# An int8 stage between the quantising VectorE step and its bf16 result, in a macaron block of feed-forward, RWKV attention and feed-forward on eight cores

## The chip, the cores and the metric

The kernel runs on one Trainium2 chip, on 8 cores at once. Each core takes one batch element: 4096 tokens of 1024 channels. The metric is the device time of the slowest core in microseconds. Every time below is one of such runs, or is read from the trace of one profiled execution of the kernel before, on core 5, the slowest of it. A core has five engines that run side by side and wait for each other through semaphores: PE (TensorE, matmul), DVE (VectorE), ACT (ScalarE), POOL (GpSimd) and SP (SyncE, which only issues transfers here). "PEld" is PE's loading of weights.

## The reference, cut to what matters

```python
x = x + 0.5 * ffn(layernorm(x), w_gate, w_up, w_down)
x = x + attn(layernorm(x), w, u, mix_k, mix_v, mix_r, Wk, Wv, Wr, Wo)
x = x + 0.5 * ffn(layernorm(x), w_gate, w_up, w_down)      # same weights as the first

def _weight_quant(w):                  # one scale for the whole matrix, values -1, 0, 1
    scale = 1.0 / clip(mean(abs(w)), 1e-05)
    return clip(round(w * scale), -1.0, 1.0) / scale
def _act_quant(x):                     # one scale per token, values -127 to 127
    scale = 127.0 / clip(max(abs(x), axis=-1), 1e-05)
    return clip(round(x * scale), -128.0, 127.0) / scale
def _bitlinear(x, w):
    return einsum('bsi,oi->bso', _act_quant(x), _weight_quant(w))
def ffn(x, w_gate, w_up, w_down):      # 1024 -> 4096 -> 1024
    return _bitlinear(silu(_bitlinear(x, w_gate)) * _bitlinear(x, w_up), w_down)
```

The attention has four projections of 1024 x 1024, a shift by one token with three mixes, and a recurrence over the tokens (running maximum, numerator, denominator). The change doesn't touch it.

## The kernel before, in words

**Weight stage, once.** For each of the three feed-forward matrices (4 M elements) there are two passes in 4 blocks of 128 partitions x 8192 elements, with two buffers `wbat`. The first pass sums the absolute values (L238). The second pass loads the blocks again and quantises each in three DVE steps: scale and clip above (L272), clip below and add 12582912 (L276; at that size an fp32 number has no digits behind the point, so the addition rounds), subtract 12582912 and write bf16 into `bbat` (L282). ACT's queue stores `bbat` to scratch. SP loads block nb only when DVE is through with block nb-2 (`vdone`), since they share a buffer. After the four blocks the matrix is transposed by DMA from scratch to scratch.

**Main part, four times** (`q` = 0 to 3, 1024 tokens each, held in `xres`): `ffn(q)`, `attn(q)`, `ffn(q)`, with a barrier of all engines behind each. In `ffn` the 1024 tokens are two tiles (`tt`) of 512 tokens, each of them 4 groups (`sub`) of 128. The order is written out by hand:

```python
quant(0)
for t in range(NTT):
    gu(t)
    if t + 1 < NTT:
        quant(t + 1)
    rounds(t)
    down(t)
```

- `quant` does the layer norm (`ln_tile`: ACT squares at L326, the rest on DVE), the maximum per token (L398), the scaling (L418) and the rounding into bf16 `xqb3` (L420: add 12582912, subtract it). `xqb3` goes to scratch, and eight DMA transposes bring it back as `xqT`.
- `gu` is the gate and up matmul (L466, L473). ACT empties PSUM (L482, L485) and POOL multiplies into `hbuf` (L491).
- `rounds` takes the maximum of `hbuf` per token (L507). Then for each of the 4 groups: scale, add 12582912 into `h05b` (L527, named `xnt_` in the trace, since it is the same memory), wait for the store of the group before (there is one `hqb`), subtract and write bf16 `hqb` (L534), store `hqb` to scratch from ACT's queue.
- `down` waits on SP for all four stores, then runs 32 chunks: a DMA transpose of 128 columns of the stored activations into `hqT`, a load of `dslab`, eight matmuls (L565). DVE adds the result to `xres` (L577).

Each engine works off its own list in order. `V.wait(V)` makes DVE wait for its own last instruction. `quant(1)` stands behind `gu(0)` in ACT's and DVE's lists and ahead of `rounds(0)`; its squares on ACT come after all the activations of `gu(0)`.

Of the kernel before, what the change touches and what calls it, by code (L numbers as in the profile page):

```python
# [9 lines left out]
I8 = mybir.dt.int8  # L10
ALU = mybir.AluOpType
ACT = mybir.ActivationFunctionType
AXX = mybir.AxisListType.X
P = 128
# [63 lines left out]
def build_nc(T=4096, C=1024, II=4096, TQ=1024, TTILE=512, ACH=256, LWc=128):  # L78
# [42 lines left out]
    with ctx:  # L121
# [88 lines left out]
            return sctx.enter_context(nc.sbuf_tensor(name, shape, dt))  # L210
        wbat = [sbt0(f"wbat{i}", [P, BELEM]) for i in range(2)]
        qbat = sbt0("qbat", [P, BELEM])
        bbat = [sbt0(f"bbat{i}", [P, BELEM], BF16) for i in range(2)]
        acc = sbt0("acc", [P, 1])
        red = sbt0("red", [P, 1])
# [3 lines left out]
        for widx, (win, scr_nat, scr_T, RR, CC2) in enumerate((  # L219
                (wg_in, scr_g, scr_gT, II, C),  # L220
                (wu_in, scr_u, scr_uT, II, C),
                (wd_in, scr_d, scr_dT, C, II))):
            BW_ = min(BELEM // CC2, RR // P)
            BN = BW_ * CC2
            NB = RR // P // BW_
            if V.c:
                nc.sync.wait_ge(V.sem, V.c)
            V.inc(nc.vector.memset(acc[:], 0.0))
            V.wait(V)
            vdone = {}  # L230
            for nb in range(NB):
                b = nb % 2
                if nb >= 2:
                    nc.sync.wait_ge(V.sem, vdone[nb - 2])
                tok = qtern.put(ap2(wbat[b], 0, BN),
                                win[nb * BW_ * P:(nb + 1) * BW_ * P, :])
                qtern.wait(V, tok)
                V.inc(nc.vector.tensor_reduce(red[:], ap2(wbat[b], 0, BN), AXX,  # L238
                                              ALU.add, apply_absolute_value=True))
                V.wait(V)  # L240
                V.inc(nc.vector.tensor_add(acc[:], acc[:], red[:]))  # L241
                V.wait(V)
                vdone[nb] = V.c
            TE.wait(V)
            TE.inc(nc.tensor.matmul(psum(7, 1, 1), acc[:], onescol[:],  # L245
                                    start=True, stop=True))
            S.wait(TE)
            S.inc(nc.scalar.activation(sca[:1, 0:1], psum(7, 1, 1), ACT.Copy,
                                       scale=1.0 / float(RR * CC2)))
            V.wait(S)  # L250
            V.inc(nc.vector.tensor_scalar_max(sca[:1, 0:1], sca[:1, 0:1], 1.0e-5))
            V.wait(V)
            V.inc(nc.vector.reciprocal(sca[:1, 1:2], sca[:1, 0:1]))
            V.wait(V)
            TE.wait(V)
            TE.inc(nc.tensor.matmul(psum(7, 2), onesrow[:], sca[:1, 0:2],
                                    start=True, stop=True))
            V.wait(TE)
            V.inc(nc.vector.tensor_copy(wsc[:, 2 * widx:2 * widx + 2], psum(7, 2)))
            V.wait(V)  # L260
            s_w_ap = wsc[:, 2 * widx + 1:2 * widx + 2]
            nc.sync.wait_ge(V.sem, V.c)
            vdone = {}
            st_toks = {}
            for nb in range(NB):
                b = nb % 2
                if nb >= 2:
                    nc.sync.wait_ge(V.sem, vdone[nb - 2])
                tok = qtern.put(ap2(wbat[b], 0, BN),
                                win[nb * BW_ * P:(nb + 1) * BW_ * P, :])  # L270
                qtern.wait(V, tok)
                V.inc(nc.vector.tensor_scalar(ap2(qbat, 0, BN),  # L272
                                              ap2(wbat[b], 0, BN),
                                              s_w_ap, 1.49, ALU.mult, ALU.min))
                V.wait(V)
                V.inc(nc.vector.tensor_scalar(ap2(wbat[b], 0, BN),  # L276
                                              ap2(qbat, 0, BN),
                                              -1.49, RMAGIC, ALU.max, ALU.add))
                V.wait(V)
                if nb >= 2 and (nb - 2) in st_toks:  # L280
                    qso.wait(V, st_toks[nb - 2])
                V.inc(nc.vector.tensor_scalar(ap2(bbat[b], 0, BN),  # L282
                                              ap2(wbat[b], 0, BN),
                                              RMAGIC, None, ALU.subtract))
                vdone[nb] = V.c
                nc.scalar.wait_ge(V.sem, V.c)
                st_toks[nb] = qso.put(scr_nat[nb * BW_ * P:(nb + 1) * BW_ * P, :],
                                      ap2(bbat[b], 0, BN))
            qso.wait_all(nc.sync)
            prev_store = [None, None]  # L290
            for cb in range(CC2 // P):
                b = cb % 2
                if prev_store[b] is not None:
                    qso.wait(nc.sync, prev_store[b])
                tok = qtr.put(ap2(trow[b], 0, RR),
                              scr_nat[:, cb * P:(cb + 1) * P], transpose=True)
                qtr.wait(nc.scalar, tok)
                prev_store[b] = qso.put(scr_T[cb * P:(cb + 1) * P, :],
                                        ap2(trow[b], 0, RR))
# [66 lines left out]
        def ffn(q):  # L366
# [9 lines left out]
            hqb = fb("hqb", [P, II], BF16)  # L376
            xnt_ = fb("xnt_", [P, NSUB, C])
            xqb3 = fb("xqb3", [P, NSUB, C], BF16)
            h05b = xnt_ if NSUB * C >= II else fb("h05b", [P, II])
            gslab = [fb(f"gslab{i}", [P, NCT, IW], BF16) for i in range(2)]  # L380
            uslab = [fb(f"uslab{i}", [P, NCT, IW], BF16) for i in range(2)]
# [7 lines left out]
            def quant(tt):  # L389
# [4 lines left out]
                if state.get("xqb_tok") is not None:  # L394
# [22 lines left out]
                sA_bc = bass.AP(sA, 0, [[NSUB, P], [1, NSUB], [0, C]])  # L417
                V.inc(nc.vector.tensor_tensor(xnt_[:], xnt_[:], sA_bc, ALU.mult))  # L418
                V.wait(V)
                V.inc(nc.vector.tensor_scalar(xqb3[:], xnt_[:], RMAGIC, RMAGIC,  # L420
                                              ALU.add, ALU.subtract))
                nc.scalar.wait_ge(V.sem, V.c)
                tok = qso.put(
                    bass.AP(sxq.tensor, 0, [[C, P], [P * C, NSUB], [1, C]]),
# [74 lines left out]
            def rounds(tt):  # L499
                alt = tt % 2  # L500
                shq = scr_hq[alt]
                if state["hq_war"][alt] is not None:
                    qtr.wait(nc.scalar, state["hq_war"][alt])
                V.wait(G)
                if state.get("hqb_tok") is not None:
                    qso.wait(V, state["hqb_tok"])
                V.inc(nc.vector.tensor_reduce(s2v[:, 0:NSUB],  # L507
                                              ap3(hbuf, 0, NSUB, II, II), AXX,
                                              ALU.max, apply_absolute_value=True))
                V.wait(V)  # L510
                V.inc(nc.vector.tensor_scalar(ln_a[:, 0:NSUB], s2v[:, 0:NSUB],
                                              1.0e-5, None, ALU.max))
                V.wait(V)
                V.inc(nc.vector.tensor_tensor(dsc[:, 0:NSUB], ln_a[:, 0:NSUB],
                                              bass.AP(wsc, 4, [[6, P], [0, NSUB]]),
                                              ALU.mult))
                V.inc(nc.vector.reciprocal(ln_b[:, 0:NSUB], ln_a[:, 0:NSUB]))
                V.wait(V)
                V.inc(nc.vector.tensor_scalar(dsc[:, 0:NSUB], dsc[:, 0:NSUB],
                                              0.5 / 127.0, None, ALU.mult))  # L520
                V.inc(nc.vector.tensor_scalar(s2v[:, 0:NSUB], ln_b[:, 0:NSUB],
                                              127.0, None, ALU.mult))
                V.wait(V)
                hq_toks = []
                for sub in range(NSUB):
                    V.wait(V)
                    V.inc(nc.vector.tensor_scalar(ap2(h05b, 0, II),  # L527
                                                  ap2(hbuf, sub * II, II),
                                                  s2v[:, sub:sub + 1], RMAGIC,
                                                  ALU.mult, ALU.add))  # L530
                    V.wait(V)
                    if hq_toks:
                        qso.wait(V, hq_toks[-1])
                    V.inc(nc.vector.tensor_scalar(hqb[:], ap2(h05b, 0, II),  # L534
                                                  RMAGIC, None, ALU.subtract))
                    nc.scalar.wait_ge(V.sem, V.c)
                    hq_toks.append(qso.put(shq[sub * P:(sub + 1) * P, :], hqb[:]))
                state["hqb_tok"] = hq_toks[-1]
                st["rounds_v"][tt] = V.c
                st["hq_toks"][tt] = hq_toks  # L540
# [358 lines left out]
```

## Time and profile before

| | us |
|---|---|
| median of 3 runs | 8913.43 |
| lowest, highest | 8907.0, 8934.02 |
| profiled execution, its own time | 8917.21 |
| its span on the slowest core (core 5) | 8915.4 |
| spans of the eight cores | 8852.0 to 8915.4 |

| engine | busy us | share of the span |
|---|---|---|
| PE, matmul | 3496.9 | 39% |
| DVE | 2724.1 | 31% |
| PE, weight load | 1556.5 | 17% |
| ACT | 1086.5 | 12% |
| POOL | 654.2 | 7% |

No engine is busy half of the time. So the shares alone don't say what bounds the kernel; it has to be read from the chain of waits and from the single stages.

### The profile page before, as it was taken

To read this page: it belongs to the slowest core of one execution; us is meant where nothing else is said; L and a number is where in the kernel's file an instruction comes from. 1 tells how busy PE (TensorE), PEld (TensorE's weight loads), DVE (VectorE), ACT (ScalarE), POOL (GpSimd) and SP (SyncE) were. 2 spreads that over 40 slices of the span, in tenths; PEclk is the share of its full clock that TensorE was granted. 3 is DMA by queue.
4 is the path that set the end of the run, shared out by engine and by line. 5 is a ranking of instruction groups with operands and counts; after the bars stand their busy time and mean duration, and the time that the engine had idled before them with its cause. 6 is when DMAs were issued, how large, how long until landed. Compare 5 with 4: busy or idle time off the path is not lost.

```text
span 8915.4 us, 49384 instructions; the slowest of 8 cores (8852.0 to 8915.4 us)
## 1 busy us (share of the span) xinstructions
PE 3496.9 (39%) x15884; PEld 1556.5 (17%) x15884; DVE 2724.1 (31%) x2918; ACT 1086.5 (12%) x1633; POOL 654.2 (7%) x524
## 2 busy tenths in 40 slices
PE   0001464233463565223463545222463545222464
PEld 0000121121121221111121212121121212121121
DVE  3342202563212201664202111565202121465201
ACT  0000110111110210111110201111110201111110
POOL 0000110001010100000110101000110101000110
PEclk9999897667887888667897888666897878666898
DMA  8885343202334243301333243301243233400243
GB/s 213 263 270 139 88 118 91 43 0 66 89 91 132 85 120 95 60 0 48 92 106 113 85 123 95 75 0 38 86 122 113 85 113 97 82 0 29 91 117 104
DMA packets 1005000, 842.20 MB, mean 94 GB/s; under 512 B 637392, under 2 KB 899536, under 8 KB 989648
## 3 DMA queue, kind: packets, MB, share of 16 engines
q1 hardware_dynamic: 969744, 671.27, 28.2%
q10 hardware_dynamic: 30528, 142.62, 4.1%
q0 software_dynamic: 4480, 25.17, 1.3%
q8 instruction: 137, 2.24, 0.1%
q14 instruction: 111, 0.91, 0.0%
HBM read 536.89 MB, written 167.77 MB: 79 GB/s over the span
## 4 chain that ended last, share of the span: by engine, by line
PE 33%; DVE 26%; DMA 21%; ACT 9%; SPq 5%; issue 4%; another core or an unknown queue 1%; DVEq 0%; ACTq 0%; POOL 0%; POOLq 0%
PE psA L466 11%; PE psA L473 10%; DMA dslab<-scr_dT 9%; PE psA L565 7%; SPq L60 5%; PE psA L711 4%; DVE s2v L507 3%; ACT gate_w L482 3%; DMA scr_hq<-hqb 3%; ACT u_w L485 3%; DVE hqb L534 2%; PE psA L828 1%; DMA uslab<-scr_uT 1%; DVE lrp L692 1%; DVE oh L753 1%
## 5 line engine op out<-in xcount | busy, mean ns | idle before, releaser
L565 PE MATMUL psA<-dslab,hqT 128*128 128x512 bf16 x4096 | 1090.9, 421 | 1760.0 <-DMA dslab<-scr_dT 1759.1
L466 PE MATMUL psA<-gslab,xqT 128*128 128x512 bf16 x4096 | 1003.7, 389 | 1392.8 <-DMA uslab<-scr_uT 755.8
L491 POOL TENSOR_TENSOR hbuf<-gate_w,u_w 128x512 f16<-128x512 f32 x512 | 648.1, 1266 | 7584.0 <-ACT u_w L485 7584.0
L473 PE MATMUL psA<-uslab,xqT 128*128 128x512 bf16 x4096 | 975.5, 381 | 0.0
L565 PEld LDWEIGHTS psA<-dslab,hqT 128*128 128x128 bf16 x4096 | 405.2, 105 | 2445.3 <-issue 2143.9
L466 PEld LDWEIGHTS psA<-gslab,xqT 128*128 128x128 bf16 x4096 | 379.6, 99 | 1991.5 <-issue 1618.1
L711 PE MATMUL psA<-xkb,wkT 128*128 128x256 bf16 x1024 | 167.5, 342 | 1309.1 <-DVE k_sb L719 759.3
L507 DVE TENSOR_REDUCE s2v<-hbuf 128x4 f32<-128x16384 f16 x16 | 275.5, 17216 | 1285.8 <-POOL hbuf L491 1285.8
L577 DVE SCALAR_TENSOR_TENSOR xres<-psA,dsc,xres 128x1024 f32<-128x1024 f32 x64 | 77.7, 1276 | 1904.9 <-PE psA L565 1904.9
L482 ACT ACTIVATE gate_w<-psA,gsc 128x512 f32<-128x512 f32 x512 | 351.8, 687 | 1761.1 <-PE psA L473 1761.0
L473 PEld LDWEIGHTS psA<-uslab,xqT 128*128 128x128 bf16 x4096 | 403.8, 99 | 494.5 <-issue 19.9
L336 DVE TENSOR_SCALAR lnv<-lnv 128x4 f32<-128x4 f32 x24 | 4.1, 170 | 1398.4 <-ACT xqb L326 1398.4
L711 PEld LDWEIGHTS psA<-xkb,wkT 128*128 128x128 bf16 x1024 | 120.7, 121 | 1359.1 <-issue 1320.9
L485 ACT ACTIVATE u_w<-psA,usc 128x512 f32<-128x512 f32 x512 | 348.2, 680 | 0.0
L482 ACT ACT_TABLE_LOAD x16 | 20.5, 1283 | 1992.6 <-PE psA L473 1992.6
L828 PE MATMUL psA<-woT,rwk 128*128 128x512 bf16 x512 | 129.7, 399 | 315.9 <-DVE stQ L816 269.6
L245 PE MATMUL psA<-onescol,acc 128*1 128x1 f32 x6 | 0.6, 163 | 602.6 <-DVE acc L241 602.6
L324 DVE TENSOR_REDUCE lnm<-xres 128x4 f32<-128x4096 f32 x24 | 106.1, 4420 | 275.2 <-DMA scr_dT<-trow 107.8
L238 DVE TENSOR_REDUCE red<-wbat 128x1 f32<-128x8192 f32 x12 | 104.2, 8686 | 237.4 <-DMA wbat<-Wu 101.5
L326 ACT ACTIVATE xqb<-xres 128x1024 bf16<-128x1024 f32 x64 | 66.7, 1047 | 845.4 <-DMA xres<-x 580.5
L711 PE MATMUL psA<-xkb,wrT 128*128 128x256 bf16 x1024 | 120.0, 277 | 16.2 <-ACT sr_sb L724 16.1
L326 ACT ACTIVATE xqb3a<-xres 128x1024 bf16<-128x1024 f32 x32 | 33.4, 1044 | 755.8 <-issue 673.6
(207 smaller groups left out, 2940.5 us busy)
## 6 DMA issues: line engine op xcount, KB each, us to landing
gslab<-scr_gT SPq DMA_DIRECT2D x128, 1024.0 KB, 5.5
uslab<-scr_uT SPq DMA_DIRECT2D x128, 1024.0 KB, 8.0
dslab<-scr_dT SPq DMA_DIRECT2D x512, 256.0 KB, 3.0
scr_hq<-hqb ACTq DMA_DIRECT2D x64, 1024.0 KB, 3.9
wbat<-Wg SPq DMA_DIRECT2D x8, 4096.0 KB, 23.2
wbat<-Wu SPq DMA_DIRECT2D x8, 4096.0 KB, 21.1
wbat<-Wd SPq DMA_DIRECT2D x8, 4096.0 KB, 20.7
xres<-x SPq DMA_DIRECT2D x4, 4096.0 KB, 13.1
```

Of the source, the lines that this page charges most:

```text
L60: inst = (self.eng.dma_start_transpose(out, in_) if transpose else self.eng.dma_start(out, in_, allow_slow_non_contiguous=slow))
L324: V.inc(nc.vector.tensor_reduce(lnm[:, 0:ns], x3, AXX, ALU.add))
L466: inst = nc.tensor.matmul(psum(bk_g, IW), ap2(xqT[alt], ct * TTILE + sub * P, P), ap2(gslab[sb_], ct * IW, IW), start=(ct == 0), stop=(ct ...
L473: inst = nc.tensor.matmul(psum(bk_u, IW), ap2(xqT[alt], ct * TTILE + sub * P, P), ap2(uslab[sb_], ct * IW, IW), start=(ct == 0), stop=(ct ...
L482: S.inc(nc.scalar.activation(gate_w[sb_][:], psum(bk_g, IW), ACT.Silu, scale=gsc2[alt][:, sub:sub + 1]))
L485: S.inc(nc.scalar.activation(u_w[sb_][:], psum(bk_u, IW), ACT.Copy, scale=usc2[alt][:, sub:sub + 1]))
L491: G.inc(nc.gpsimd.tensor_mul(ap2(hbuf, sub * II + iw * IW, IW), gate_w[sb_][:], u_w[sb_][:]))
L507: V.inc(nc.vector.tensor_reduce(s2v[:, 0:NSUB], ap3(hbuf, 0, NSUB, II, II), AXX, ALU.max, apply_absolute_value=True))
L534: V.inc(nc.vector.tensor_scalar(hqb[:], ap2(h05b, 0, II), RMAGIC, None, ALU.subtract))
L565: inst = nc.tensor.matmul(psum(sub * NCW + cw, CW), ap2(hqT[hb], sub * P, P), ap2(dslab[hb], cw * CW, CW), start=(ic == 0), stop=(ic == NI ...
L711: inst = nc.tensor.matmul(psum(bank, ACH), ap2(wt, ct * C + dch * P, P), ap2(xkb3, mi * NCT * ACH + ct * ACH, ACH), start=(ct == 0), stop= ...
L828: inst = nc.tensor.matmul(psum(bank, CW), ap2(rwk, ct * ACH + tsub * P, P), ap2(woT, ct * C + cw * CW, CW), start=(ct == 0), stop=(ct == N ...
```

## The change

At each of the three places where a rounded value is written as bf16, the DVE instruction now writes int8, DVE waits for it, and a second DVE instruction (`tensor_copy`, in the profile a CAST) turns int8 into bf16. Three int8 buffers are new (8, 4 and 4 KB per partition). The stores still read bf16, so every transfer is the same.

```diff
+        ibat = sbt0("ibat", [P, BELEM], I8)
@@ weight stage
+                V.inc(nc.vector.tensor_scalar(ap2(ibat, 0, BN), ap2(wbat[b], 0, BN),
+                                              RMAGIC, None, ALU.subtract))
+                V.wait(V)
                 if nb >= 2 and (nb - 2) in st_toks:
                     qso.wait(V, st_toks[nb - 2])
-                V.inc(nc.vector.tensor_scalar(ap2(bbat[b], 0, BN), ap2(wbat[b], 0, BN),
-                                              RMAGIC, None, ALU.subtract))
+                V.inc(nc.vector.tensor_copy(ap2(bbat[b], 0, BN), ap2(ibat, 0, BN)))
                 vdone[nb] = V.c
@@ ffn
+            xqi3 = fb("xqi3", [P, NSUB, C], I8)
+            hqi = fb("hqi", [P, II], I8)
@@ quant
-                V.inc(nc.vector.tensor_scalar(xqb3[:], xnt_[:], RMAGIC, RMAGIC,
+                V.inc(nc.vector.tensor_scalar(xqi3[:], xnt_[:], RMAGIC, RMAGIC,
                                               ALU.add, ALU.subtract))
+                V.wait(V)
+                V.inc(nc.vector.tensor_copy(xqb3[:], xqi3[:]))
@@ rounds
                     if hq_toks:
                         qso.wait(V, hq_toks[-1])
-                    V.inc(nc.vector.tensor_scalar(hqb[:], ap2(h05b, 0, II),
+                    V.inc(nc.vector.tensor_scalar(hqi[:], ap2(h05b, 0, II),
                                                   RMAGIC, None, ALU.subtract))
+                    V.wait(V)
+                    V.inc(nc.vector.tensor_copy(hqb[:], hqi[:]))
                     nc.scalar.wait_ge(V.sem, V.c)
```

DVE's list in the first `rounds` before, where `eV` is DVE's own counter and `qo0` to `qo3` are the counters of ACT's store queue:

```order
L527 TENSOR_SCALAR xnt__1<-hbuf,s2v 128x4096 [waits eV]
L534 TENSOR_SCALAR hqb<-xnt__1 128x4096 [waits eV]
L527 TENSOR_SCALAR xnt__1<-hbuf,s2v 128x4096 [waits eV]
L534 TENSOR_SCALAR hqb<-xnt__1 128x4096 [waits eV,qo2]
L527 TENSOR_SCALAR xnt__1<-hbuf,s2v 128x4096 [waits eV]
L534 TENSOR_SCALAR hqb<-xnt__1 128x4096 [waits eV,qo3]
```

The same place now (lines are those of the changed kernel: 542 was 534, 535 was 527):

```order
L535 TENSOR_SCALAR xnt__1<-hbuf,s2v 128x4096 [waits eV]
L542 TENSOR_SCALAR hqi<-xnt__1 128x4096 [waits eV]
L545 CAST hqb<-hqi 128x4096 [waits eV]
L535 TENSOR_SCALAR xnt__1<-hbuf,s2v 128x4096 [waits eV]
L542 TENSOR_SCALAR hqi<-xnt__1 128x4096 [waits eV,qo2]
L545 CAST hqb<-hqi 128x4096 [waits eV]
```

The wait for the store of the group before (`qo2`) stands ahead of the int8 instruction, where it stood ahead of the bf16 one; the CAST comes behind both.

DVE's list in the second pass of the first matrix, the last two blocks, now:

```order
L273 TENSOR_SCALAR qbat<-wbat,wsc 128x8192 [waits qt2]
L277 TENSOR_SCALAR wbat<-qbat 128x8192 [waits eV]
L281 TENSOR_SCALAR ibat<-wbat 128x8192 [waits eV]
L287 CAST bbat<-ibat 128x8192 [waits eV,qo0]
L273 TENSOR_SCALAR qbat<-wbat,wsc 128x8192 [waits qt3]
L277 TENSOR_SCALAR wbat<-qbat 128x8192 [waits eV]
```

Before, a block was the three instructions L272, L276 and L282, and L282 wrote `bbat` with the wait for `qo0`. `qt2` is the load of the block.

## Rows read from the trace of the kernel before

**Rows 1.** The page, part 4: shares of the chain that ended last.
```profile
PE 33%; DVE 26%; DMA 21%; ACT 9%; SPq 5%; issue 4%; another core or an unknown queue 1%; DVEq 0%; ACTq 0%; POOL 0%; POOLq 0%
```

**Rows 2.** Who waited for whom: total us, times, longest us.
```profile
DVE lnv L336 <- ACT xqb L326: 1398.4, 8, 176.8
PE psA L565 <- DMA dslab<-scr_dT: 1759.1, 362, 82.9
```

**Rows 3.** Chain, 740 to 870 us (start, us, what): a `quant(0)`.
```profile
822.96 2.30 DVE xqb L420
825.39 5.26 DMA scr_xq<-xqb
```

**Rows 4.** Chain, 1028 to 1092 us: end of the first `rounds`.
```profile
1080.02 3.89 DMA scr_hq<-hqb
1084.03 1.11 SPq L60
```

**Rows 5.** Timeline of DVE, 1018 to 1120 us: start, us, instruction, [idle before].
```profile
1035.09 2.29 DVE L420 TENSOR_SCALAR xqb<-xnt__1 128x4096 bf16<-128x4096 f32 x1
1037.30 17.21 DVE L507 TENSOR_REDUCE s2v<-hbuf 128x4 f32<-128x16384 f16 x1
...
1058.12 2.29 DVE L534 TENSOR_SCALAR hqb<-xnt__1 128x4096 bf16<-128x4096 f32 x1
1060.52 2.35 DVE L527 TENSOR_SCALAR xnt__1<-hbuf,s2v 128x4096 f32<-128x4096 f16 x1
1064.76 2.29 DVE L534 TENSOR_SCALAR hqb<-xnt__1 128x4096 bf16<-128x4096 f32 x1 [1.88 <-DMA scr_hq<-hqb]
```

**Rows 6.** Line L534: what DVE sat idle for before it, us, times.
```profile
  DMA scr_hq<-hqb: 81.5, 48
```

**Rows 7.** DVE's groups: names, shapes, count | busy us, mean ns | idle before.
```profile
L238 DVE TENSOR_REDUCE red<-wbat 128x1 f32<-128x8192 f32 x12 | 104.2, 8686 | 237.4 <-DMA wbat<-Wu 101.5 <-DMA wbat<-Wd 101.4 <-DMA wbat<-Wg 34.5
L534 DVE TENSOR_SCALAR hqb<-xnt__1 128x4096 bf16<-128x4096 f32 x8 | 18.4, 2294 | 10.5 <-DMA scr_hq<-hqb 10.3
L398 DVE TENSOR_REDUCE sA<-xnt__1 128x4 f32<-128x4096 f32 x2 | 8.8, 4420 | 0.2
L672 DVE COPY xnT<-xnbound 128x8 bf16<-128x8 bf16 x4 | 0.7, 185 | 82.9 <-DMA xnT<-scr_xn 82.9
```

**Rows 8.** Stretches: us, busy us of each engine (count), granted PE clock, DMA share, GB/s.
```profile
1008.00:1085.00 77.00, 0.00 (x0) 0.00 (x0) 58.26 (x32) 5.84 (x11) 1.26 (x1) 0.52 0.23 82
1085.00:1100.00 15.00, 8.92 (x23) 3.09 (x24) 0.00 (x0) 0.00 (x0) 0.00 (x0) 0.61 0.46 105
1100.00:1200.00 100.00, 58.92 (x218) 21.62 (x216) 0.00 (x0) 0.00 (x0) 0.00 (x0) 0.91 0.47 105
```

**Rows 9.** Timeline, first matrix (176 to 305 us): second pass.
```profile
179.06 4.49 DVE L272 TENSOR_SCALAR qbat<-wbat,wsc 128x8192 f32<-128x8192 f32 x1 [16.63 <-DMA wbat<-Wg]
...
192.53 4.48 DVE L272 TENSOR_SCALAR qbat<-wbat,wsc 128x8192 f32<-128x8192 f32 x1
...
215.38 4.49 DVE L272 TENSOR_SCALAR qbat<-wbat,wsc 128x8192 f32<-128x8192 f32 x1 [9.30 <-DMA wbat<-Wg]
...
232.91 4.49 DVE L272 TENSOR_SCALAR qbat<-wbat,wsc 128x8192 f32<-128x8192 f32 x1 [3.91 <-DMA wbat<-Wg]
...
242.10 4.43 DVE L282 TENSOR_SCALAR bbat<-wbat 128x8192 bf16<-128x8192 f32 x1 [0.17 <-DVE wbat L276]
```

**Rows 10.** Timeline of DVE: blocks 2 and 3 of the second matrix.
```profile
438.70 4.49 DVE L272 TENSOR_SCALAR qbat<-wbat,wsc 128x8192 f32<-128x8192 f32 x1 [9.00 <-DMA wbat<-Wu]
...
454.91 4.49 DVE L272 TENSOR_SCALAR qbat<-wbat,wsc 128x8192 f32<-128x8192 f32 x1 [2.58 <-DMA wbat<-Wu]
```

**Rows 11.** Timeline of DVE: blocks 2 and 3 of the third matrix.
```profile
658.83 4.49 DVE L272 TENSOR_SCALAR qbat<-wbat,wsc 128x8192 f32<-128x8192 f32 x1 [9.07 <-DMA wbat<-Wd]
...
673.97 4.49 DVE L272 TENSOR_SCALAR qbat<-wbat,wsc 128x8192 f32<-128x8192 f32 x1 [1.52 <-DMA wbat<-Wd]
```

**Rows 12.** Stretch between blocks 0 and 3, first matrix; columns as in rows 8.
```profile
192.70:232.90 40.20, 0.00 (x0) 0.00 (x0) 26.50 (x6) 0.00 (x0) 0.00 (x0) 1.00 0.96 333
```

More of the change, by code:

```diff
@@ L279, in build_nc @@
                 V.wait(V)
+                V.inc(nc.vector.tensor_scalar(ap2(ibat, 0, BN),
+                                              ap2(wbat[b], 0, BN),
+                                              RMAGIC, None, ALU.subtract))
+                V.wait(V)
                 if nb >= 2 and (nb - 2) in st_toks:
                     qso.wait(V, st_toks[nb - 2])
-                V.inc(nc.vector.tensor_scalar(ap2(bbat[b], 0, BN),
-                                              ap2(wbat[b], 0, BN),
-                                              RMAGIC, None, ALU.subtract))
+                V.inc(nc.vector.tensor_copy(ap2(bbat[b], 0, BN),
+                                            ap2(ibat, 0, BN)))
                 vdone[nb] = V.c
```

## The prediction
> **What bounds the kernel now.** I read the chain of work that ended last first, since the shares of busy time name no engine. It is a chain that passes from engine to engine: PE 33%, DVE 26%, DMA 21%, ACT 9% [rows 1]. So the stages run one behind the other, and a microsecond added on DVE counts fully wherever DVE is the only one at work and not at all where it waits anyway. The question for each of the three places is which of the two holds.
>
> The waits come second. Before `rounds(0)`, DVE sits in L336 for ACT's squares, 8 times, up to 176.8 us [rows 2]: these are the `quant(1)` of the 8 feed-forward calls, which can't start before `gu(0)` is through. So `quant(1)` hides under no matmul. PE's L565 (`down`) waits for `dslab`, at the longest 82.9 us in one go [rows 2]: that is PE standing through `quant(1)` and `rounds(0)`.
>
> The chain by time comes third. A `quant(0)` is on it: L420, then at once the store of `xqb3` [rows 3]. At the end of `rounds` the last store is on it and SP's first transpose directly behind it [rows 4]. The timeline of DVE shows the same from inside: L507 starts as soon as L420 is done, and in `rounds` the second L534 starts when the store of the first has landed, 1.88 us after DVE was free [rows 5]. From 1008 to 1085 us PE has no instruction at all and POOL one; DVE works 58.26 of the 77 us [rows 8].
>
> **The change, part by part.** Counts first: 12 added CASTs of 8192 elements in the weight stage (3 matrices of 4 blocks), 16 of 4096 in `quant` (4 q, 2 calls, 2 tiles), 64 of 4096 in `rounds` (16 tiles of 4 groups). Nothing is removed; one instruction at each place changes its output from bf16 to int8.
>
> *Cost of one added CAST.* No row shows int8, so this is bounded from both sides. The nearest rows are the one-input instructions whose input and output differ in type: fp32 to bf16, 4096 elements, 2294 ns [rows 7], fp16 to fp32, 2.35 us [rows 5], and fp32 to bf16, 8192 elements, 4.43 us [rows 9]. The slow end is the rate of the reductions, 4420 ns for 4096 and 8686 for 8192 [rows 7], half as fast. The other end is the smallest COPY, 185 ns for 8 elements [rows 7]. I take 2.29 us and 4.43 us: three pairs of widths already run at the faster rate, so mixed widths do not by themselves cost it. For the int8 write I take the same duration as for the bf16 write, so no change there; its slow end is 4.42 as well, 2.13 us more.
>
> What these widths are worth is also told by the Trainium skill, Vector Engine (DVE) Microarchitecture Reference, section 5.1: two results per cycle through both ports ask for one source, both sides in SBUF and an even count, and name no type; four ask for two-byte types on both sides. By that rule CAST and int8 write stay at the faster of the two rates seen and reach no higher one, which is the value taken above; the trace agrees for the pairs it has and shows no byte type.
>
> *Start to start.* The dependent pair L534 and L527 starts 60.52 - 58.12 = 2.40 us apart for 2.29 us of work [rows 5], so a CAST that waits for the instruction ahead costs 2.29 + 0.11 = 2.40 us, and 4.43 + 0.11 = 4.54 us at 8192.
>
> Here a rule of the skill speaks for more. VectorE: DVE Perf Modes, section "The DRAIN you can't avoid", says that each instruction is followed by a flush of about its duration less 266 ns before the next can start. By it, the added instructions of 4096 would cost some 4.3 us each. The rows disagree: L420 to L507 is 2.21 us, and L534 to L527 2.40 [rows 5].
>
> *rounds: 64 x 2.40 = 153.6 us.* Can the CAST lie beside the store of the group before? No: the wait for that store now stands ahead of the int8 write, and the CAST follows that. The period of a group before is 1064.76 - 1058.12 = 6.64 us, made of L534 (2.3), the issue and the store (4.1); L527 lies beside the store [rows 5]. All 48 later groups wait like this, 81.5 us in total [rows 6]. After, it is int8 write, CAST, store: 2.40 more, and the idle 1.7 us stays. The first group and the last are plain DVE time ahead of a store, too. ACT's queue, which waits for DVE before each store, holds nothing else at this time; SP waits for the fourth store, and PE for SP. So all 64 are on the path.
>
> *quant: 16 x 2.40 = 38.4 us.* In the 8 `quant(0)` the store follows L420 on the chain [rows 3], and PE can't start before it. In the 8 `quant(1)` the L507 of `rounds(0)` is next on DVE and its input is long there [rows 5]; the transposes of `xqT` move 2.4 us, but have the 17.21 us of L507 as cover.
>
> *Weight stage: 34 us.* Let a block be q = 192.53 - 179.06 = 13.47 us [rows 9]; it becomes 13.47 + 4.54 = 18.01. Loads of block 2 and 3 are released by the ends of block 0 and 1. Block 2 then starts 4.54 later. Block 3 starts when block 2 ends, or when its load lands. First matrix: block 2 ends at 215.38 + 4.54 + 18.01 = 237.93, 5.0 behind the old start of block 3 (232.91); its load, released 9.1 later, lands 4.5 to 9.1 later, depending on whether the DMA was full (share 0.96 [rows 12]) or not. So block 3 starts 5.0 to 9.1 later and takes 4.54 longer: 9.6 to 13.6. Second matrix, by the same sum from [rows 10]: 438.70 + 22.55 - 454.91 = 6.3, so 10.9 to 13.6. Third [rows 11]: 658.83 + 22.55 - 673.97 = 7.4, so 11.9 to 13.6. Together 32.4 to 40.9. I take 34, near the low end, since the DMA share was 0.96: the load gains what the queue ahead of it loses. Everything behind (store, transposes, first layer norm) starts later by as much. POOL has nothing to do in that stretch [rows 12].
>
> *At nothing:* the PE clock. PE's rest gets longer by 12 us before `down(0)` (one `quant`, four groups). But the granted clock is 0.52 already, the 1.2 GHz level, over the rest of 77 us, 0.61 in the 15 us behind it and 0.91 later [rows 8]; a rest that is already cold is only made longer. Without that cover it would be a few matmuls at half the clock, under 3 us per call. The transfers are the same in number and size.
>
> **Sum.** 153.6 + 38.4 + 34 = 226 us. Against the profiled execution's own 8917.2 us (span 8915.4) that is 9143; the median shown is 4 lower, 8913.4, so I forecast 9140 us.
>
> **Rivals.**
> 1. *One of the two int8 instructions runs at the reductions' rate* (write or read, not both). Then each of the 80 costs 2.40 + 2.13 = 4.53 us: 362. A weight block becomes 13.47 + 4.54 + 4.26 = 22.3 us, DVE is hardly waiting any more, the four take 89 us instead of 67.5 (179.06 to 246.53 [rows 9]), 22 more, 65 for three matrices. Sum 427: 9340 us. For it: no byte type in any row. Against it: the rate doesn't care for the three pairs of widths seen. The flush of the page above would land close by, at roughly 80 x 4.3 + 12 blocks' share, again some 9320 us; it shares this chance, of which the rows leave it little.
> 2. *Both at that rate.* 80 x 6.66 = 533; a block becomes 26.5 us, four 106, 39 more, 117 for three: 650. That gives 9563 us.
> 3. *The CAST is twice as fast as taken.* From 2294 and 4427 ns a fixed part of 161 and 0.521 ns per element follow; half the slope gives 1.23 us, with the gap 1.34. 80 x 1.34 = 107, and the weights some 18: 125, or 9038 us. No row runs at such a rate. The extreme end, the 185 ns of the smallest COPY, would be 80 x 0.30 = 24 and next to nothing in the weights, 8938 us.
> 4. *Not slower: `down` gives it back.* PE waits 1759.1 us for `dslab` [rows 2]; 8 waits of about 83 are `rounds(0)` with its `quant`, and 8 are `rounds(1)` without one, shorter by the 29 us from 1008 to the start of L507 at 1037.30 [rows 5], so about 54 each; some 660 remain for the 512 chunks, 1.3 us each. If cores that share memory drifted apart by the longer DVE phases and met less in `down`, chunks could shorten. It would have to be 226 / 512 = 0.44 us per chunk to come out at 8913, and decides only from there. Against it: all eight cores get the same delay at the same places, and the DMA share in `down` is 0.47 [rows 8], far from full, so latency and not bandwidth sets the chunk.
> 5. *The change does nothing.* The order of instructions has 92 more on DVE, so this is out.
>
> **How the numbers follow.** Forecast 84%; rival 1 with the flush 9%; rival 2 2%; rival 3 3%; rival 4 2%. In the forecast's case the size rests on 192 us that are nearly rigid, 32 to 41 in the weight stage, and about 0.3% (27 us) between executions, either way; that gives 9098 to 9190 with 95% of the 84, so 80% in all, and reaching on to 9340 is not needed. A difference under 0.3% is what a measurement of this kernel can't tell from none. Faster 1%, same 1%, slower 98% (half of rival 4 would still lie within the 0.3%, half beyond).
>
> **What would show it.** In the profile after: CAST `hqb<-hqi` x64 and CAST `xqb<-xqi` x16 of 2.29 us, CAST `bbat<-ibat` x12 of 4.43, and the three int8 writes unchanged at 2.29 and 4.43. The period of a group in `rounds` goes from 6.4 or 6.6 to 8.8 or 9.0 us with the idle time before the int8 write still about 1.7 us. `down` and `gu` keep their lengths. In the weight stage DVE's wait before block 3 is gone or nearly so. What would make it wrong: a duration of 4.4 us at any int8 row, chunks of `down` that change by over 0.1 us, or a wait of the CAST for something other than its own engine.

## The result, and the profile after

| | before | changed |
|---|---|---|
| median of 8 runs, us | 8915.68 | 9127.03 |
| lowest, highest, us | 8903.88, 8955.52 | 9123.02, 9134.04 |
| ratio, 95% interval | | 1.0232, 1.0217 to 1.0248 |
| profiled execution: spans of the cores, us | 8852.0 to 8915.4 | 9051.1 to 9147.5 |

The change makes the kernel slower by 211 us in the medians; the interval of the ratio is worth 193 to 221 us. The forecast was 9140 us, 226 us more than its own base, so it is right in mechanism and some 15 us high. The rows below are of core 1, the slowest of the changed kernel's profiled execution, which took 9149.21 us and so lies above the eight timed ones; those of before are of core 5.

DVE's groups in the changed kernel (line, names, shapes, count, busy us, mean ns, idle before):

```profile
L545 DVE CAST hqb<-hqi 128x4096 bf16<-128x4096 int8 x64 | 146.8, 2294 | 7.0 <-DVE hqi L542 0.5
L281 DVE TENSOR_SCALAR ibat<-wbat 128x8192 int8<-128x8192 f32 x12 | 53.1, 4427 | 1.3
L287 DVE CAST bbat<-ibat 128x8192 bf16<-128x8192 int8 x12 | 53.1, 4427 | 1.6 <-DVE ibat L281 1.0
L429 DVE CAST xqb<-xqi 128x4096 bf16<-128x4096 int8 x16 | 36.7, 2294 | 1.6
L542 DVE TENSOR_SCALAR hqi<-xnt__1 128x4096 int8<-128x4096 f32 x8 | 18.4, 2294 | 10.5 <-DMA scr_hq<-hqb 10.3
```

The int8 writes take 2294 and 4427 ns, as the bf16 writes did [rows 7], and the CASTs take the same. So beside the fp32-to-bf16 instructions of before, a byte type on either side changes nothing.

The timeline of DVE in the first `rounds`, where [rows 5] shows the old one:

```profile
1092.73 2.29 DVE L545 CAST hqb<-hqi 128x4096 bf16<-128x4096 int8 x1
1095.13 2.35 DVE L535 TENSOR_SCALAR xnt__1<-hbuf,s2v 128x4096 f32<-128x4096 f16 x1
1099.27 2.29 DVE L542 TENSOR_SCALAR hqi<-xnt__1 128x4096 int8<-128x4096 f32 x1 [1.78 <-DMA scr_hq<-hqb]
1101.66 2.29 DVE L545 CAST hqb<-hqi 128x4096 bf16<-128x4096 int8 x1
1104.06 2.35 DVE L535 TENSOR_SCALAR xnt__1<-hbuf,s2v 128x4096 f32<-128x4096 f16 x1
1108.14 2.29 DVE L542 TENSOR_SCALAR hqi<-xnt__1 128x4096 int8<-128x4096 f32 x1 [1.72 <-DMA scr_hq<-hqb]
```

The CAST starts 2.39 us after the int8 write. The idle time for the store is still there, 1.7 to 1.8 us. The period from one int8 write to the next is 8.87 us, where it was 6.4 to 6.6. In the list of waits the store's share is nearly unchanged (81.5 us before [rows 6]), while PE waits longer ahead of `down` and in it (1759.1 us before, at the longest 82.9 [rows 2]):

```profile
DVE hqi L542 <- DMA scr_hq<-hqb: 80.2, 48, 1.8
PE psA L575 <- DMA dslab<-scr_dT: 1932.2, 353, 94.3
```

Between these two cores PE's wait grew by 173.1 us. On the mean of the eight cores the 16 long waits ahead of `down` grew from 1087.9 to 1260.6 us, by 172.7, and the short ones inside `down` went from 653.5 to 657.9. The 64 CASTs in `rounds` and the 8 in `quant(1)`, at 2.40 us each, make 172.8. So they all show up as a later start of `down`, and its chunks are as long as before.

The stretches around the first `rounds` (columns as in [rows 8], which they answer):

```profile
1039.50:1122.00 82.50, 0.00 (x0) 0.00 (x0) 69.83 (x37) 3.83 (x8) 0.00 (x0) 0.50 0.19 64
1122.00:1137.00 15.00, 5.53 (x16) 1.95 (x16) 0.00 (x0) 0.00 (x0) 0.00 (x0) 0.60 0.43 140
1137.00:1237.00 100.00, 61.41 (x232) 22.71 (x232) 0.00 (x0) 0.00 (x0) 0.00 (x0) 0.91 0.47 116
```

PE has nothing to do while DVE works, and its granted clock is at the low level there (0.50), 0.60 just behind and 0.91 later, as before (0.52, 0.61, 0.91). No cost of the longer rest is to be seen in the clock here.

The second pass of the first weight matrix (answering [rows 9]), and block 3 of the second (answering [rows 10]):

```profile
178.89 4.49 DVE L273 TENSOR_SCALAR qbat<-wbat,wsc 128x8192 f32<-128x8192 f32 x1 [16.25 <-DMA wbat<-Wg]
...
196.89 4.48 DVE L273 TENSOR_SCALAR qbat<-wbat,wsc 128x8192 f32<-128x8192 f32 x1
...
218.45 4.49 DVE L273 TENSOR_SCALAR qbat<-wbat,wsc 128x8192 f32<-128x8192 f32 x1 [3.48 <-DMA wbat<-Wg]
...
236.99 4.49 DVE L273 TENSOR_SCALAR qbat<-wbat,wsc 128x8192 f32<-128x8192 f32 x1 [0.39 <-DMA wbat<-Wg]
...
250.71 4.43 DVE L287 CAST bbat<-ibat 128x8192 bf16<-128x8192 int8 x1 [0.17 <-DVE ibat L281]
```

```profile
448.43 4.49 DVE L273 TENSOR_SCALAR qbat<-wbat,wsc 128x8192 f32<-128x8192 f32 x1 [1.73 <-DMA wbat<-Wu]
...
466.69 4.49 DVE L273 TENSOR_SCALAR qbat<-wbat,wsc 128x8192 f32<-128x8192 f32 x1
```

The pass now takes 255.14 - 178.89 = 76.25 us where it took 67.47. The wait before block 3 has gone from 3.91 and 2.58 us to 0.39 and none on these cores. On the mean of the eight cores it went from 4.69, 4.02 and 3.85 us (first, second and third matrix) to 1.18, 1.38 and 1.46, and the pass from 66.5, 65.4 and 65.8 us to 76.0, 74.9 and 75.2.

To see where the 211 us lie, I added up the stages for each core from the timelines of DVE and took the mean over the eight cores of the one profiled execution of each kernel (up to DVE's last instruction, 14 us before the end of the span in both):

| stage, us, mean of the cores | before | changed | difference | forecast |
|---|---|---|---|---|
| weight stage, to the first layer norm | 785.8 | 816.7 | +30.9 | +34 |
| 8 `quant(0)` | 240.0 | 258.4 | +18.4 | +19.2 |
| 8 `gu(0)` with `quant(1)` | 1688.7 | 1705.1 | +16.4 | +19.2 |
| 16 `rounds` | 678.8 | 831.7 | +152.9 | +153.6 |
| 8 `gu(1)` | 1315.8 | 1318.1 | +2.3 | 0 |
| 16 `down` | 1870.8 | 1870.5 | -0.3 | 0 |
| the rest (attention, load and store of x) | 2281.5 | 2274.0 | -7.5 | 0 |

One execution is a small sample. Over the fourteen kernels profiled, a stage that the edits leave alone differs by this much from one to the next: the weight stage by 6 us, `gu(0)` by 6, `down` by 25, the rest by 15, `quant(0)` and `rounds` by 1 to 2.

### The profile page after: what moved, and what is told of

The parts are those of the page before. It is cut to its first block, busy times and chain, and to the rows that moved or that the text cites. A ratio compares the mean times of both kernels' runs of the same rounds, so it can differ in the third digit from the quotient of the medians.

```text
span 9147.5 us, 49568 instructions; the slowest of 8 cores (9051.1 to 9147.5 us)
## 1 busy us (share of the span) xinstructions
PE 3499.0 (38%) x15884; PEld 1556.8 (17%) x15884; DVE 2961.2 (32%) x3010; ACT 1087.3 (12%) x1633; POOL 654.5 (7%) x524
## 4 chain that ended last, share of the span: by engine, by line
PE 33%; DVE 28%; DMA 20%; ACT 8%; SPq 6%; issue 4%; another core or an unknown queue 1%; DVEq 0%; ACTq 0%; POOL 0%; POOLq 0%
PE psA L474 11%; PE psA L481 10%; DMA dslab<-scr_dT 9%; PE psA L575 7%; SPq L60 5%; PE psA L721 4%; DVE s2v L515 3%; ACT gate_w L490 3%; DMA scr_hq<-hqb 3%; ACT u_w L493 3%; DVE hqi L542 2%; DVE hqb L545 2%; PE psA L838 1%; DMA uslab<-scr_uT 1%; DVE lrp L702 1%
## 5 line engine op out<-in xcount | busy, mean ns | idle before, releaser
L545 DVE CAST hqb<-hqi 128x4096 bf16<-128x4096 int8 x64 | 146.8, 2294 | 7.0 <-DVE hqi L542 0.5
```

Of the source, the lines that this page charges most:

```text
L545: V.inc(nc.vector.tensor_copy(hqb[:], hqi[:]))
```

## The experiments

Each was timed beside the kernel before on the same chip. They ran on three chips in all, and the changed kernel wasn't timed again beside them, so a difference in medians from it, or between kernels of two chips, also holds the difference of the chips; where it matters the difference of the ratios is given too. A difference in us is between the medians if nothing else is said; where one execution's stages are given they are the means of the eight cores, made as in the table above.

**The parts alone.** Three kernels, each the kernel before with the hunks of one place.

*Weight stage alone*: `ibat` and its two instructions.

> Only the weight stage has the int8 write and the CAST; quant and rounds are as before. Theory (two DVE instructions in a row, each at the rate of the old one, cost 4.54 us per block where DVE is late, and the load of block 3 gives part of it back): 27 to 34 us above the kernel before, ratio 1.003 to 1.004, from the profile of the changed kernel (8.8, 8.4 and 10.3 us longer per matrix). Rival (the stage is bound by DMA at its end, so nothing is seen): 0 to 10 us. Rival (the stage had more to lose than its four blocks show, and the shortfall of the forecast lies in the feed-forward parts): 40 us.

Measured: ratio 1.0037 (1.0019 to 1.0055), +40 us in the medians, +33 by the ratio. The weight stage is 31.2 us longer (817.0 us). The theory holds, and DMA does not hide the work. The times alone leave room for the rival of 40 us (the interval is worth 17 to 49 us); the stage, 31.2 us longer, doesn't.

*quant alone*: `xqi3` and its two instructions.

> Only quant has the int8 write and the CAST (16 of 4096 elements). Theory: all 16 lie on the path, 16 x 2.40 = 38 us above the kernel before, ratio 1.0043. Rival (quant(1) lies beside the matmuls after all, only the 8 quant(0) count): 19 us, ratio 1.002. Rival (the shortfall of 15 us of the forecast lies here, in the next wait): 23 us.

Measured: ratio 1.0036 (1.0019 to 1.0053), +32 us by the ratio, +38 in the medians. The times don't decide, since 19 us still lies in the interval (17 to 47 us). The stages do: `quant(0)` is 18.4 us longer and `gu(0)` with `quant(1)` 16.2, so all 16 count.

*rounds alone*: `hqi` and its two instructions.

> Only rounds has the int8 write and the CAST (64 of 4096 elements). Theory: 64 x 2.40 = 154 us above the kernel before, ratio 1.0172, the group's period 8.8 to 8.9 us, and the 32 chunks of down as long as before. Rival (down gives part back, since its transfers meet other traffic less): 110 to 140 us, with chunks shorter. The three parts together should give what the changed kernel gives, 211 us, if they don't interact.

Measured: 9078.43 us, ratio 1.0177 (1.015 to 1.0204), +158 us. `rounds` is 833.2 us in sum, +154.4; `down` 1861.9. So `down` gives nothing back that can be told from its own spread: over the profiled executions of kernels in which it is the same it ran from 1855 to 1880 us. The interval is worth 134 to 182 us and so just touches the rival's 110 to 140; the stages don't support it. The three ratios add up to 1.0250, the whole change gave 1.0232: no interaction is seen.

**What the width of a type does.** The same number of instructions, but two bytes on both sides of the second one.

```diff
-            xqi3 = fb("xqi3", [P, NSUB, C], I8)
-            hqi = fb("hqi", [P, II], I8)
+            xqi3 = fb("xqi3", [P, NSUB, C], BF16)
+            hqi = fb("hqi", [P, II], BF16)
```

> The changed kernel with the buffers between of quant and rounds as bf16 in place of int8 (weight stage unchanged, int8), so the same number of instructions, the second one a bf16 to bf16 copy. Theory (it is the number of two-byte operands that sets the rate; both sides two bytes wide run at twice the rate, 1.23 us for 4096 elements): 80 x 1.07 = 85 us below the changed kernel, about 9042 us, ratio to before 1.0142. Rival (a second pass costs 2.29 us whatever its type): 9127 us, ratio 1.023. Rival (the copy is faster but the path is then set by something else, such as a store): between the two.

Measured: 9039.57 us, ratio 1.0143 (1.0116 to 1.017), 87 us below the changed kernel (79 by the ratios; 85 were expected). Its DVE groups:

```profile
L545 DVE COPY hqb<-hqi 128x4096 bf16<-128x4096 bf16 x64 | 78.5, 1227 | 6.9 <-DVE hqi L542 0.5
L429 DVE COPY xqb<-xqi 128x4096 bf16<-128x4096 bf16 x16 | 19.6, 1227 | 1.6
```

The copy takes 1227 ns in place of 2294. The rate that rival 3 of the prediction used exists on this chip, for two bytes on both sides, and the byte type doesn't reach it. The rule of the Trainium skill quoted in the prediction (Vector Engine (DVE) Microarchitecture Reference, section 5.1) says just this, and the runs agree in both halves.

**The place of the wait.** In the changed kernel, the wait for the store of the group before goes from ahead of the int8 write to behind it.

```diff
-                    if hq_toks:
-                        qso.wait(V, hq_toks[-1])
                     V.inc(nc.vector.tensor_scalar(hqi[:], ap2(h05b, 0, II),
                                                   RMAGIC, None, ALU.subtract))
                     V.wait(V)
+                    if hq_toks:
+                        qso.wait(V, hq_toks[-1])
                     V.inc(nc.vector.tensor_copy(hqb[:], hqi[:]))
```

> The changed kernel with the wait for the store of the group before moved from ahead of the int8 write to behind it, ahead of the CAST (the int8 buffer isn't read by the store, so this is free). Theory: the int8 write then fills the 1.7 us that DVE sat idle, and the period of a group is set by DVE alone, 2.35 + 2.29 + 2.29 + 3 x 0.11 = 7.3 us, in place of 8.85: 48 x 1.6 = 75 us below the changed kernel, about 9052 us, ratio to before 1.015. Rival (the store sets the period whatever stands ahead of it): 9127 us, ratio 1.023.

Measured: 9079.88 us, ratio 1.0184 (1.016 to 1.0207), 47 us below the changed kernel (43 by the ratios). The timeline has the period that the theory said, 1121.66 - 1114.34 = 7.32 us, and no wait for a store:

```profile
1114.34 2.29 DVE L540 TENSOR_SCALAR hqi<-xnt__1 128x4096 int8<-128x4096 f32 x1
1116.81 2.29 DVE L545 CAST hqb<-hqi 128x4096 bf16<-128x4096 int8 x1 [0.17 <-DVE hqi L540]
1119.20 2.35 DVE L535 TENSOR_SCALAR xnt__1<-hbuf,s2v 128x4096 f32<-128x4096 f16 x1
1121.66 2.29 DVE L540 TENSOR_SCALAR hqi<-xnt__1 128x4096 int8<-128x4096 f32 x1
```

The sixteen `rounds` fall from 831.7 to 761.0 us, 71 of the 75 expected. Of these 71 the median shows 47. In the same execution the weight stage and `down` were 4 us longer each and the rest 3, which the edit doesn't touch; what is left is open, within an interval of the ratio that is 42 us wide.

The same with two buffers `hqb` in turn:

> As the kernel with the wait behind the int8 write, and two buffers hqb in turn, so that the CAST waits only for the store of two groups before. Theory: DVE was no longer late for the store there, so the period stays 7.3 us: 9050 us, the same as with one buffer, ratio 1.015. Rival (the CAST still waited some for the store): up to 20 us less.

Measured: 9062.23 us, ratio 1.016 (1.0134 to 1.0185). The median is 18 us lower than with one buffer, as the rival would have it, but the two intervals of the ratio overlap, and `rounds` is 759.9 us against 761.0. So a second buffer behind the moved wait brings `rounds` no more than 1 us.

**The same cover without int8.** The kernel before with two buffers `hqb`. The diff shows the main lines alone; DVE also waits for the stores of both buffers ahead of L507, where it waited for the one.

```diff
+                    hqb = hqb2[sub % 2]
-                    if hq_toks:
-                        qso.wait(V, hq_toks[-1])
+                    if sub >= 2:
+                        qso.wait(V, hq_toks[sub - 2])
```

> The kernel before (no int8) with two buffers hqb in turn. Theory: the wait of L534 for the store goes; the period of a group falls from 6.4 to 6.6 us to 2.35 + 2.29 + 2 x 0.11 = 4.86 us: 48 x 1.65 = 79 us below the kernel before, about 8835 us, ratio 0.991. Rival (stores now meet each other and the last lands later, so SP starts no earlier): 0 to 30 us. Another rival (down is held by something else that ran out during the waits): no change.

Measured: 8832.19 us, ratio 0.9908 (0.9886 to 0.993), 79 us below the kernel before; `rounds` 606.8 us, 72 less. DVE has no wait for a store left. The group behind the rows below has a period of 4.93 us, where 4.86 was expected. The 5.29 in the rows themselves has one late start of L527 (0.46 us idle), which comes only twice on this core; its cause isn't shown.

```profile
1063.20 2.35 DVE L527 TENSOR_SCALAR xnt__1<-hbuf,s2v 128x4096 f32<-128x4096 f16 x1
1065.65 2.29 DVE L535 TENSOR_SCALAR hqb<-xnt__1 128x4096 bf16<-128x4096 f32 x1
1068.41 2.35 DVE L527 TENSOR_SCALAR xnt__1<-hbuf,s2v 128x4096 f32<-128x4096 f16 x1 [0.46 <-DVE hqb L535]
1070.94 2.29 DVE L535 TENSOR_SCALAR hqb<-xnt__1 128x4096 bf16<-128x4096 f32 x1 [0.17 <-DVE xnt__1 L527]
```

**Release of the weight buffer.** The weight stage alone, with the release of `wbat` moved ahead of the CAST.

```diff
                                               RMAGIC, None, ALU.subtract))
+                vdone[nb] = V.c
                 V.wait(V)
...
                                             ap2(ibat, 0, BN)))
-                vdone[nb] = V.c
```

> Only the weight stage has the int8 write and the CAST, and SP is released to load the next block as soon as the int8 write is done, since the CAST doesn't read wbat. Theory (the loads of blocks 2 and 3 are released by blocks 0 and 1): load 2 is released as early as before, load 3 4.5 us later; DVE itself, 18 us a block, then sets the pace: 4.5 us per block for blocks 1 to 3, less the 9 and 2 to 4 us that DVE waited ahead of blocks 2 and 3; per matrix about 5 to 9 us, so 15 to 27 us above the kernel before, ratio 1.002 to 1.003, below the 27 to 34 of the version that releases at the CAST. Rival (DVE's own time sets the stage already, release is indifferent): the same as that version, ratio 1.0037.

Measured: ratio 1.0023 (1.0008 to 1.0039), +21 us by the ratio; the weight stage 811.1 us, 5.9 less than with the late release. The intervals of the two ratios overlap, so the timed runs don't tell the theories apart. The 5.9 us are no larger than what such a stage differs by from one execution to the next. The trace does decide: blocks 1, 2 and 3 now start without a wait, and the pass takes 72.2 us for every matrix on every core, against 75.0 to 76.3 with the late release (mean of the cores):

```profile
195.77 4.48 DVE L273 TENSOR_SCALAR qbat<-wbat,wsc 128x8192 f32<-128x8192 f32 x1
...
213.76 4.48 DVE L273 TENSOR_SCALAR qbat<-wbat,wsc 128x8192 f32<-128x8192 f32 x1
...
231.82 4.48 DVE L273 TENSOR_SCALAR qbat<-wbat,wsc 128x8192 f32<-128x8192 f32 x1
```

**The CAST on another engine.** In the changed kernel, the CAST of `rounds` goes to ACT, with two buffers of each kind. The diff shows the main lines alone; DVE also waits, ahead of the int8 write, for ACT's CAST of two groups before.

```diff
-                    V.wait(V)
-                    V.inc(nc.vector.tensor_copy(hqb[:], hqi[:]))
+                    S.wait(V)
+                    if sub >= 2:
+                        qso.wait(S, hq_toks[sub - 2])
+                    S.inc(nc.scalar.activation(hqb[:], hqi[:], ACT.Copy))
```

> The changed kernel with the CAST of rounds (int8 to bf16, 64 times) on ACT in place of DVE, two int8 and two bf16 buffers in turn. Theory (the CAST costs what it does because it stands in DVE's list, not as work): DVE's period of a group falls to 4.86 us; ACT needs about 3.6 us for 4096 elements (four times the 0.85 us slope of its 1024-element squares, plus the start), so it follows DVE and only the last one of a tile is added: 4 x 4.86 + 3.6 = 23.0 us per tile against 4 x 7.33 = 29.3 with the CAST on DVE and two buffers: 16 x 6.3 = 100 us below that one's 9062, about 8960 us, ratio 1.005. Rival (two engines hand over slowly or ACT is slower on int8): 9000 us or more.

Measured: 8969.23 us, ratio 1.007 (1.0045 to 1.0095). The 64 CASTs still run and are slower one by one, yet the kernel is 93 us faster than with two buffers and the CAST on DVE (80 by the ratios; 100 were expected). `rounds` falls from 759.9 to 666.8 us, which is 93 too. ACT's rows:

```profile
1102.49 3.62 ACT L550 ACTIVATE hqb<-hqi 128x4096 bf16<-128x4096 int8 x1 [1.24 <-DVE hqi L545]
...
1107.48 3.62 ACT L550 ACTIVATE hqb<-hqi 128x4096 bf16<-128x4096 int8 x1 [1.37 <-DVE hqi L545]
```

ACT waits for DVE, not DVE for ACT.

**The place of quant(1).** The kernel before with `quant(1)`'s computing ahead of `gu(0)` in the lists; its store and transposes stay behind. The diff shows the order of the calls alone; `quant_out` holds the store and the transposes that stood at the end of `quant`.

```diff
             quant(0)
+            quant_out(0)
             for t in range(NTT):
-                gu(t)
                 if t + 1 < NTT:
                     quant(t + 1)
+                gu(t)
+                if t + 1 < NTT:
+                    quant_out(t + 1)
```

> The kernel before (no int8), with the computing part of quant(1) put ahead of gu(0) in the lists of ACT and DVE, and its store and transposes left behind gu(0). Theory (quant(1) was on the path only by its place behind gu(0) in ACT's list): L507 starts when POOL has its last product, 27 us earlier in 8 places: 220 us below the kernel before, about 8693 us, ratio 0.975. Rival (DVE's long two-port instructions and POOL's products, now at the same time, hold each other up, or ACT is late for the first PSUM banks): 100 to 180 us.

Measured: 8677.01 us, ratio 0.9741 (0.97 to 0.9782), 235 us below the kernel before. `gu(0)` with `quant(1)` falls from 1688.7 to 1468.4 us, by 220.3, which is the theory's 220. `gu(1)` is 14 us shorter as well, which the theory didn't have; its cause is open. DVE is through with the second L417 (L420 before) long ahead of L511 (L507 before), which starts behind POOL:

```profile
838.22 2.29 DVE L417 TENSOR_SCALAR xqb<-xnt__1 128x4096 bf16<-128x4096 f32 x1
992.46 17.22 DVE L511 TENSOR_REDUCE s2v<-hbuf 128x4 f32<-128x16384 f16 x1 [151.95 <-POOL hbuf L495]
```

Then with int8 and the CAST in `quant`:

> The same as the one with quant(1) early, and with the int8 write and the CAST in quant alone (16 times). Theory (what a CAST costs depends on its place): the 8 in quant(0) cost 19 us, the 8 in quant(1) nothing, so 19 us above the version with quant(1) early and no int8, about 8712 us, ratio 0.977; behind gu(0) the same 16 CASTs cost 32 to 38 us. Rival (both cost, place is indifferent): 38 us above.

Measured: 8708.2 us, ratio 0.9765 (0.9725 to 0.9805), 31 us above the version without int8 (21 by the ratios). That lies between theory (19) and rival (38), and the intervals overlap, so the time doesn't decide. The stages do: `quant(0)` 258.7 against 240.3 us, +18.4; `gu(0)` with `quant(1)` 1465.6 against 1468.4, so not longer at all. In all the mean of the cores is 35 us longer in this execution; beside the 16 us of these two stages, the weight stage is longer by 4, `down` by 14, `gu(1)` by 5 and `rounds` by 2 and the rest is shorter by 5, all places that the edit doesn't touch. With `quant(1)` under the matmuls its CASTs are free.

Both gains together:

> The kernel before with quant(1) early and two buffers hqb, so the two gains together, no int8. Theory (they lie in different places and add up): 220 + 79 us below the kernel before, about 8615 us, ratio 0.967. Rival (SP's transposes of xqT for the second tile, now behind gu(0) with less cover, hold down up): 20 to 60 us more.

Measured: 8612.43 us, ratio 0.9671 (0.9629 to 0.9712), 299 us below the kernel before and 515 below the changed one (500 by the ratios). It is the fastest of all versions, and the gains add up (235 + 79 = 314, against 299).

## Why the prediction was right, and where it was off

- *Price of a CAST and of the int8 write.* Taken as 2.29 and 4.43 us, measured 2.29 and 4.43. Rivals 1 and 2 fall with that, rival 3 too, and the bf16 copy shows what rival 3 would have needed. The flush that the Trainium skill states (VectorE: DVE Perf Modes, "The DRAIN you can't avoid") is seen in no run here: the int8 write and the CAST start 2.39 us apart.
- *All 64 in `rounds` are on the path.* Held: +152.9 against 153.6. Shown by the part alone (+158 by the ratio), by the same CASTs on ACT, by the moved wait, which wins back what an instruction hides beside the store, and by PE's longer wait. One reading was loose: the period of 6.64 us was made up of 2.3 and 4.1, which is 6.4, the period of the later groups.
- *All 16 in `quant` are on the path.* Held in kind: 34.8 in the stages against 38.4, 32 by the ratio of the part alone. The shortfall is no larger than what the stages differ by between executions: with `quant` untouched, `quant(0)` was 239.1 and 239.4 us in two of the parts alone, which would make 19 us of its 18.4. The 8 in `quant(1)` are there only because of their place, which the early `quant(1)` shows.
- *Weight stage, 34.* Measured 30.9, of which the second passes add 28.4 (mean of the cores), below the low end of 32.4. Two things in the term were off. First, it was read from core 5 alone, which waited less before block 3 than the others. The same sum, done for each core from its own trace and averaged, has its low end at 29.4. Second, the step "block 2 then starts 4.54 later" failed. Behind the start of block 0, block 2 started 36.32 us before and 39.56 now, 3.2 later on the cores shown, and 3.3 on the mean of cores and matrices. Its load took 21.2 us from issue to landing, where it had taken 22.5. Load 3 took 21.8 where it had taken 26.6; it landed 4.2 later, just under the 4.5 to 9.1 of the prediction, and block 3 waited for it, 0.39 us on the core shown and 1.2 to 1.5 on the mean, and did not start as soon as block 2 was done. A likely reason, argued and not tried alone, is that load 3 and store 1 now start 18 us and not 13.5 behind load 2, so the loads share the DMA for less of their time. The early release fits it: there load 2 starts 4.5 us ahead of store 0 and took 19.5 us.
- *The PE clock costs nothing.* Held in the stretch that was looked at, 0.50, 0.60, 0.91.
- *Rival 4, `down` gives it back.* Refuted: 1870.8 and 1870.5 us in `down`, and 653.5 and 657.9 us of waits in its chunks, where 226 us would have had to go.
- *The sum.* 226 against 211 (193 to 221). About 3 us of the 15 are the weight stage and 4 `quant`. Some 7 were in stages that the change doesn't touch (the rest, -7.5), which ran from 2272 to 2287 us over all the kernels profiled; that is no effect of the change, and that it brought the time down and not up is chance. The range of 9098 to 9190 held, with the measured time in its lower half. Its stated terms (192, 32 to 41, and 27 either way, on 8913) give only 9110 to 9173; the time lies in that as well.

## What to carry to other kernels

An added instruction costs its time only where its engine is the one that the others wait for, and its place in that engine's list decides more than its length: the same CAST cost about 2 us behind `gu(0)` (16.4 us for 8) and nothing ahead of it, and 64 slower ones on an idle engine cost less than 64 on the busy one. When a stage stands in the chain of waits with a single engine at work, look for what could move out of it before counting what is in it; here that gave 235 us, and 299 together with a second buffer for the store, where the change had cost 211. A wait belongs ahead of the first instruction that needs it and not ahead of the one before.

## What the runs showed of the hardware

With `quant(1)` beside POOL's products, an instruction of DVE and one of POOL hold each other up. First DVE's rows, then POOL's, from the version with early `quant(1)` and int8:

```profile
857.85 2.29 DVE L418 TENSOR_SCALAR xqi<-xnt__1 128x4096 int8<-128x4096 f32 x1
860.25 3.17 DVE L421 CAST xqb<-xqi 128x4096 bf16<-128x4096 int8 x1
```

```profile
859.25 2.02 POOL L498 TENSOR_TENSOR hbuf<-gate_w,u_w 128x512 f16<-128x512 f32 x1 [855.49 <-ACT u_w L492]
864.41 1.26 POOL L498 TENSOR_TENSOR hbuf<-gate_w,u_w 128x512 f16<-128x512 f32 x1 [3.15 <-ACT u_w L492]
```

POOL's product begins while L418 runs and takes 2.02 us in place of 1.26; the CAST begins while the product runs and takes 3.17 us in place of 2.29. In the kernel before no product took over 1.27 us; here the longest on this core took 3.24. The Trainium skill (SBUF — State Buffer, "Who interferes with whom") says that the two share a pair of ports, held for a whole instruction, and the rows fit that: each of the two ends about as late as if it had begun when the other one ended. Here it costs nothing that the stages show (`gu(0)` is no longer than without int8). Where POOL was the late engine, a CAST hidden under its work would cost POOL time; no run here tries that.
